# Last attention's first unit: order of transfers on the SyncE queue, and place of the first turn of row maxima

## What is computed

```python
qkv = (x @ W_qkv).reshape(Bx, Nx, 3, H, D)
q, k, v = (qkv[:, :, 0], qkv[:, :, 1], qkv[:, :, 2])
...
sim = (qg_n[None, None] * q_n).sum(-1).mean(-1)      # one number per token
sim = (sim - sim.min()) / (sim.max() - sim.min())
pos = sim > 0.9                                       # class of a token
logits = jnp.einsum('bqhd,bkhd->bhqk', q * scale, k)
...                                                   # softmax over the tokens of one class
reg_out = (x_pos[:, :REG] + x_neg[:, :REG]) * 0.5     # 5 register tokens see both classes
tok_out = jnp.where(pos[:, :, None, None], x_pos[:, REG:], x_neg[:, REG:])
...
return out @ W_proj + b_proj
```

## Time and profile before

| | us |
|---|---|
| median of three executions | 1333.91 |
| lowest, highest | 1333.17, 1338.76 |
| the profiled execution's own time | 1333.7 |
| its span | 1332.0 |
| TensorE busy | 1215.1 (91%) |
| VectorE busy | 1000.7 (75%) |
| ScalarE busy | 835.3 (63%) |
| GpSimd busy | 227.5 (17%) |

### The profile page before, as it was taken

How to read it: one execution, slowest core, us unless ns; L and a number is a source line. 1 busy time by engine, 2 the same in 40 slices (tenths; PEclk the granted TensorE clock), 3 DMA queues, 4 the chain that set the end, 5 groups by cost and what they waited for, 6 DMA issues and landing times.

```text
span 1332.0 us, 26359 instructions
## 1 busy us (share of the span) xinstructions
PE 1215.1 (91%) x10562; PEld 565.5 (42%) x10562; DVE 1000.7 (75%) x1491; ACT 835.3 (63%) x1484; POOL 227.5 (17%) x176
## 2 busy tenths in 40 slices
PE   4989974999999898879999999999999999999988
PEld 3566762555567455343233232332232333333247
DVE  4895695665536758368999999999999999999602
ACT  1224573777742742115887878887788877888861
POOL 2130124554741423710000000000000000000000
PEclk9878985999999999888999999999999999999989
DMA  6100027557500334722323443144332543233003
GB/s 189 26 1 15 1 31 137 121 108 136 96 1 1 119 119 135 134 35 48 56 62 64 87 72 63 47 82 84 56 68 56 87 78 59 56 70 50 2 1 126
DMA packets 78825, 92.55 MB, mean 69 GB/s; under 512 B 15210, under 2 KB 53356, under 8 KB 78704
## 3 DMA queue, kind: packets, MB, share of 16 engines
q1 hardware_dynamic: 78704, 90.87, 33.7%
HBM read 67.02 MB, written 23.80 MB: 68 GB/s over the span
## 4 chain that ended last, share of the span: by engine, by line
PE 60%; DVE 27%; ACT 5%; issue 2%; SPq 2%; DMA 2%; POOL 1%; DVEq 0%; ACTq 0%; POOLq 0%
DVE sm L2093 19%; PE ps L1560 10%; PE ps L1551 9%; PE ps L1532 6%; ACT W L1022 3%; PE ps L1322 2%; PE ps L1670 2%; PE ps L1416 2%; PE ps L1313 2%; PE ps L1314 2%; PE ps L1375 2%; PE ps L1542 1%; PE ps L1280 1%; PE ps L1278 1%; PE ps L1331 1%
## 5 line engine op out<-in xcount | busy, mean ns | idle before, releaser
L1022 ACT ACTIVATE W<-ps 128x512 f32<-128x512 f32 x1024 | 534.8, 605 | 140.6 <-PE ps L1560 136.7
L2093 DVE TENSOR_REDUCE sm<-ps 128x1 f32<-128x1024 f32 x512 | 599.3, 1217 | 29.7 <-PE ps L1532 26.3
L1560 PE MATMUL ps<-R 99*32 99x512 bf16 x4096 | 319.2, 384 | 5.5 <-ACT W L1022 3.2
L1551 PE MATMUL ps<-W,R 128*32 128x512 f32 x2048 | 265.5, 594 | 0.7 <-ACT W L1022 0.7
L1560 PEld LDWEIGHTS ps<-R 99*32 99x32 bf16 x4096 | 86.1, 94 | 225.2 <-ACT W L1022 167.0
L803 POOL COPY R<-R 128x512 f32<-128x512 f32 x16 | 9.7, 613 | 629.5 <-PE ps L1551 625.9
L1532 PE MATMUL ps<-R 50*128 50x512 bf16 x512 | 89.9, 390 | 17.7 <-DVE sm L2093 15.0
L1532 PE MATMUL ps<-KM,R 50*128 50x512 bf16 x512 | 87.3, 384 | 9.6 <-DVE sm L2093 6.6
L945 ACT ACTIVATE R<-ps 77x512 f32<-77x512 f32 x128 | 75.1, 592 | 23.5 <-PE ps L1314 14.2
L1551 PEld LDWEIGHTS ps<-W,R 128*32 128x32 f32 x2048 | 63.0, 111 | 42.2 <-ACT W L1022 1.4
L1872 DVE TENSOR_REDUCE small<-ps 128x4 bf16<-128x308 f32 x128 | 57.5, 472 | 23.2 <-PE ps L1280 23.1
(11 more groups left out here) (262 smaller groups left out, 1576.0 us busy)
## 6 DMA issues: line engine op xcount, KB each, us to landing
R<-x_parts SPq DMA_DIRECT2D x96, 128.0 KB, 4.8
R<-q_parts SPq DMA_DIRECT2D x192, 64.0 KB
R<-q_parts SPq DMA_DIRECT2D x96, 128.0 KB
R<-k_parts SPq DMA_DIRECT2D x96, 128.0 KB
x_parts<-R SPq DMA_DIRECT2D x8, 768.0 KB, 7.0
q_parts<-R SPq DMA_DIRECT2D x24, 256.0 KB, 2.6
k_parts<-R SPq DMA_DIRECT2D x24, 256.0 KB, 2.6
X<-in_x SPq DMA_DIRECT2D x4, 1024.0 KB, 9.8
```

The source lines that it names most:

```text
L1022: act.activation(PR[:, s % 2, h, :], third_bank("score", 64 * u + n), ACT.Exp, scale=0.25).then_inc(s_sfree, 1)
L1551: mm = pe.matmul(bank(7)[32 * h:32 * h + 32, :], VST[j][:, k, h, :], PR[:, s % 2, h, :], start=(k == 0), stop=(k == TB - 1))
L1560: mm = pe.matmul(o[32 * c:32 * c + 32, :], KST[j][0:MAX_ROW + 1, h, t:t + 32], QST[j][0:MAX_ROW + 1, h, 512 * (s // 8):512 * (s // 8) + 51 ...
L2093: dve.tensor_reduce(MX[:, half, h, q:q + 1], bank(2 * ((p + 1) % 2), 2), AX, ALU.max).then_inc(s_tfree, 1)
```

## The change

The write of key chunk 5 moves on SyncE from ahead of the class rows to behind the load of `crow`. In the prologue the turn ("rows", 0) moves from behind tile 15 to behind tile 17, which is behind register values and register sum of batch 2; SyncE waits for 19 turns instead of 17 before it stores the row. The rows turn's own wait on TensorE is set to 16 turns, fewer than `take_pair(18)` waits for.

```diff
-        LEAD = 6
+        LEAD, ROW_LAG = 6, 2
         PROLOGUE, left = [], list(range(32 - LEAD))
 
         def add_tiles(n):
             for a in left[:n]:
                 PROLOGUE.append(("tile", a))
-                if a == 15:
+                if a == 15 + ROW_LAG:
                     PROLOGUE.append(("rows", 0))
             del left[:n]
...
             load_max_parts(0, 0)
-            for c in range(3, 6):
+            for c in range(3, 5):
                 write_qk(KP, c, s_kl, s_kw2)
             sp.wait_ge(s_sc2, CLS_DONE)
             for k in (2, 0, 1, 3):
...
             sp.dma_start(crow.rearrange("p (b t) -> p b t", b=B),
                          CR[2, :, 0, :].unsqueeze(0)).then_inc(s_crl, 16)
-            write_qk(KP, 6, s_kl, s_kw2)
+            for c in range(5, 7):
+                write_qk(KP, c, s_kl, s_kw2)
             sp.wait_ge(s_clw, 16 * 3 * B)
             load_max_class_rows(0, 0)
             write_qk(KP, 7, s_kl, s_kw2)
...
-            store_row(0, 0, s_tfree, 17, 0)
+            store_row(0, 0, s_tfree, 17 + ROW_LAG, 0)
...
                     else:
                         o = take_pair(n)
-                        pe.wait_ge(s_tfree, n)
+                        pe.wait_ge(s_tfree, 16)
                         max_rows(o, arg)
```

## The result

The changed kernel takes **1321.88 us** (median of 6, 1320.49 to 1322.17) against 1334.03 (median of 6) for the kernel before: ratio 0.990, 95% interval 0.9883 to 0.9918. Two more series on other chips gave 0.9911 [0.9896, 0.9925] and 0.9916 [0.9902, 0.9931]. Between the medians it is faster by 12.2 us here, and by 11.1 and 10.5 us in the other two series. The forecast was 1325.6 with a range from 1322.3: the sign is right, the size too small.

A forecast was written before the change was run, and what follows sets the result against it. TensorE, busy 91%, was taken as the bound, with stalls of 4.06 us for `crow` and 1.96 us at the rows turn. Terms 3.21 + 1.56 + 2.33 + 1.6 - 0.6 = 8.1 us gave 1325.6 us, range 1322.3 to 1330.5.

The forecast's parts named there:

- The wait for `crow`, 3.21 us: TensorE ahead of batch 0's register scores: class DMAs and `crow` come earlier, so these scores start 3.21 us earlier.
- The clock behind that wait, 1.56 us: Batch 0's register scores: with 0.85 us idle instead of 4.06 they run warmer, 5.33 us instead of 6.89.
- The late write: Chunk 5's write, some 5 us later, delays chunk 7's cast and batch 0's exponentials; covered by 0.5 us, costs nothing.
- Part two: Rows turn two tiles later, from tile 15 to unit 0's first scores: 2.33 + 1.6 - 0.6 = 3.3 us gained.
- The slip of 0.6: Between the maxima of tiles 17 and 18: the moved rows turn takes a PSUM pair, delaying tile 18, minus 0.6 us.
- Their length: Register values of batch 2, 5.71 us before: a clock gain of 0.8 to 2.45 us, middle taken, 1.6 us.
- Theory M: Posed for the experiments, not the prediction: outside the clock, the change moves more than was counted; no size given.
- the sum I drew from it, 1327.2: Whole kernel: by the skill's rule the clock term of register values belongs to no kernel; gain 6.5 us, 1327.2.
- the clock giving nothing: Rival 1, TensorE's clock: slow stretches only move to other products; 4.9 us remain, 1328.8; chance 0.22.
- the write as bound: Rival 2: chunk 5's late write holds chunk 7's cast and register scores 1; 2.6 us lost, 1328.2; chance 0.12.
- the order doing nothing: Rival 3, SyncE's order: something else holds `crow`, only part two's 3.3 us remains, 1330.4; chance 0.04.
- the clock staying low in unit 0's scores: Rival 4, slower: TensorE stays at 1.2 GHz in unit 0, costing up to 21 us, 1347; chance 0.03.

The follow-up runs named there:

- The filler: Kernel before with 16 bf16 128x512 products nobody reads put into TensorE's wait for `crow`, wait not shortened: ratio 0.9971 [0.9955, 0.9987] against 1334.77.
- Order only: Kernel before with only chunk 5's write moved behind the load of `crow`, rows turn left where it was: 1330.73 us, ratio 0.9955 [0.9938, 0.9972].

## Why the prediction was right in kind and short in size

**The wait for `crow`, 3.21 us:** right. It measured 3.67 to 3.76 in the traces; 0.5 us of it are the class DMAs, issued in 5.47 us instead of 5.97; they took 5.94 to 5.97 in all six traces with the write in front and 5.46 or 5.47 in all seven without it; why is not shown.

**The clock behind that wait, 1.56 us: this is the step that failed, by size.** I took the difference of two rows of one trace, register scores of batch 0 against those of batch 1, as all that the idle stretch costs, and put register values of batch 0 at nothing. The filler, which takes away the clock's part and leaves the wait, gave 3.9 us (1.7 to 6.0). Over the four traces with the stall, the section from register scores 0 to tile 15 averages 52.05 us (50.45 to 56.83), and 47.2 without it in seven of nine: besides the 1.6 us, slow register values of batch 0 (1.4 to 1.6 us more) stood in every trace with the stall, and once the slow stretch ran through the value projection as well and batch 1's register values were slow too. I put batch 0's slow register values down as given, the same before and after; it went away in all traces of the changed kernel. "Order only" is the exception: its one trace has no stall, and yet register values of batches 0 and 1 take 4.5 and 4.9 us. So falls can come without the stall. That it brings more of them on the whole rests on the filler's series and on seven traces of nine.

**The late write, nothing, with 0.5 us of cover:** right to 0.03 us.

**Part two.** The start of register values, 2.33 us: right, 0.32 us behind tile 15. The slip of 0.6: right, 581.85 to 588.67 is 6.82 us, against 6.23 (592.95 to 599.18) before. Their length: I took 1.6 us, the middle; it is 4.9 us in all three traces of after, so 0.8, the lower end. But 2.77 us is the difference of one pair. Over the traces of the second table the section takes 22.3 us on average (20.6 to 24.6) behind tile 15 and 19.3 behind tile 17: 3.0 us, so the 3.3 of the forecast was about right, while its clock term varies from trace to trace (register values of batch 2 took 4.5 to 6.1 us in the old order without fillers). The series gives 5.2 us (2.9 to 7.6), which holds this; its surplus is not settled. The row's later store was covered: no trace of the changed kernel has a wait for a DMA at the first scores.

**The rest.** In the first pair 1.04 us ahead of the change and 2.34 behind the bodies helped the changed kernel. Both are scatter: over all thirteen traces the start up to L2024 takes 520.8 to 524.9 us and the last stretch 70.8 to 73.2, and neither goes with the sort of kernel. So the size of the first pair's gain is in part luck.

The measured terms are 3.7 + 3.9 + 3.0 = 10.6 us, against 10.5, 11.1 and 12.2 us between the medians of the three series, within what the intervals allow. Theory M is left with the 0.5 us of the class DMAs; what else may be missing is not traced to one place. The rule of the Trainium skill weighed in the prediction ("TensorE: Matmul & The Clock Gate", Part 1: slow stretches meet the kernel at differing places) is borne out in part: the two traces of the kernel before have slow stretches of other length and place (10.54 and 15.34 us for one section, batch 1's register values slow in one only), while the three traces of the changed kernel all have the slow register values in batch 2. But the sum I drew from it, 1327.2, went the wrong way: by the filler's run slow time goes away with the stall, and not only to another place.

The rivals: the clock giving nothing is refuted by the filler; the write as bound stood 0.5 us off and was not met; the order doing nothing is refuted by "order only" and by the wait, 0.32 us for 4.06; the clock staying low in unit 0's scores did not come, unit 0 took 35.87 us for 35.95, and 35.7 to 37.3 over all traces of either sort.

## What to carry to other kernels

A transfer that nobody needs yet, issued ahead of one that an engine waits for, costs its own wait for data, not only its issue time: read what releases the queue's entries. Where TensorE idles for some microseconds in the middle of dense work, count the stall and then again what runs behind it at 1.2 GHz, and bound that from several traces: here it cost about as much as the stall itself (3.9 us, between 1.7 and 6.0, and 3.7). A filler in a wait is a cheap test of it, and in this place also a cure; in a sparse stretch, where the clock fell as the fillers began, it gave nothing.

## What was not expected of the hardware

After an idle stretch of 4.06 us the granted clock was back by 538 in one execution, and after one of 3.59 us at the same place it stayed at 0.50 for some 14 us in another (534.9 to 548.5), with no idle time of TensorE in its rows. And removing one slow stretch with three fillers (register values of batch 2, 4.9 to 3.3 us) was followed by one in the next batch, which had been free of them.
